# Ten output groups of the second layer turned back from channel rows instead of straight into token rows

## What is computed

```python
# first layer
xm = x * rsqrt(mean(x*x) + 1e-6) * rms_w * (1 + scale) + shift      # scale, shift = cond @ w_cond
q, k, v = split(xm @ w_qkv);  q, k = rope(q), rope(k)
x = softmax(q k^T / 4) v @ w_out + x
# second layer
xn = layer_norm(x) * norm_w + norm_b
q, k, v = xn @ q_w + q_b, xn @ k_w + k_b, (xn @ v_w + v_b) * mask
y = softmax(q k^T + (mask - 1) * 1e6) v
e = silu(cond) @ emb_w + emb_b
h = layer_norm(y) * sb_w + sb_b, times (1 + scale), plus shift
x = x + silu(h) @ out_w + out_b
```

## Time and profile before

| what | value |
|---|---|
| median of 3 runs | 493.06 us (492.68 to 494.52) |
| profiled execution, its own time | 493.28 us |
| its span in the trace | 491.5 us |
| PE, DVE, ACT, POOL busy | 479.5, 386.1, 342.7, 314.2 us |
| granted clock of PE | full speed in all 40 slices |

### The profile page before, as it was taken

One profiled execution on the slowest core, in us unless ns is written; L12 is line 12 of the kernel. 1 busy time (PEld: TensorE's weight loads), 2 busy tenths in 40 slices (PEclk: granted clock), 3 DMA queues, 4 the chain that ended last, 5 costly groups with the idle time before them and its releaser, 6 DMA issues.

```text
span 491.5 us, 9721 instructions
## 1 busy us (share of the span) xinstructions
PE 479.5 (98%) x3205; PEld 178.4 (36%) x3205; DVE 386.1 (79%) x990; ACT 342.7 (70%) x676; POOL 314.2 (64%) x447
## 2 busy tenths in 40 slices
PE   7999899999999999999999999999999999999996
PEld 3563322323333334333343234333333323333234
DVE  3767896998886688856887688967899999999224
ACT  1662467898767786867767776776787778777853
POOL 6569976888798898699737692739991055005501
PEclk9999999999999999999999999999999999999999
DMA  7775157444423365225412361104411121111011
GB/s 244 197 206 194 45 135 264 112 115 149 112 66 115 111 183 149 68 68 140 123 54 67 107 187 44 46 24 126 114 45 44 45 88 45 44 45 45 2 43 43
DMA packets 41577, 49.79 MB, mean 101 GB/s; under 512 B 12388, under 2 KB 34036, under 8 KB 41272
## 3 DMA queue, kind: packets, MB, share of 16 engines
q1 hardware_dynamic: 33336, 31.84, 22.6%
q0 software_dynamic: 7904, 16.03, 10.9%
q10 hardware_dynamic: 288, 1.31, 0.8%
HBM read 27.62 MB, written 19.01 MB: 95 GB/s over the span
## 4 chain that ended last, share of the span: by engine, by line
PE 79%; DVE 14%; issue 3%; POOL 2%; ACT 1%; DVEq 0%; POOLq 0%; ACTq 0%
PE bank L602 20%; PE bank L648 12%; PE bank L576 11%; PE bank L585 11%; PE bank L564 9%; DVE masked L958 8%; PE bank L659 6%; PE bank L676 5%; DVE row_max L961 2%; PE bank L633 2%; ACT probs L787 1%; PE bank L617 1%; PE bank L610 1%; PE bank L734 1%; POOL shift L1335 1%
## 5 line engine op out<-in xcount | busy, mean ns | idle before, releaser
L787 ACT ACTIVATE probs<-bank 128x512 f32<-128x512 f32 x512 | 270.2, 599 | 71.3 <-PE bank L576 70.6
L961 DVE TENSOR_REDUCE row_max<-bank 128x1 f32<-128x512 f32 x256 | 159.9, 681 | 38.1 <-PE bank L585 37.9
L585 PE MATMUL bank<-k_s,q_s 64*128 64x512 f16 x512 | 179.9, 382 | 2.1 <-DVE row_max L961 1.2
L958 DVE CUSTOM_DVE_ANT_0 masked<-bank,mask_bias 128x512 bf16<-128x512 f32 x256 | 162.1, 687 | 20.3 <-PE bank L585 19.6
L564 PE MATMUL bank<-q_s,k_s 64*128 64x512 f16 x512 | 151.3, 380 | 0.3
L576 PE MATMUL bank<-shift,kx 64*128 64x512 f16 x512 | 148.7, 376 | 0.0
L602 PE MATMUL bank<-probs,v_aug 128*17 128x512 f32 x1024 | 135.4, 598 | 0.7 <-ACT probs L787 0.7
L585 PEld LDWEIGHTS bank<-k_s,q_s 64*128 64x128 f16 x512 | 46.2, 93 | 154.6 <-DVE row_max L961 67.4
L1238 POOL TENSOR_SCALAR scaled<-row_max 128x16 f32<-128x16 f32 x30 | 7.7, 256 | 86.3 <-DVE row_max L958 49.0
L648 PE MATMUL bank<-xT,wqkv 128*128 128x512 f32 x128 | 59.6, 605 | 1.0 <-DVE xT L1095 0.6
L576 PEld LDWEIGHTS bank<-shift,kx 64*128 64x128 f16 x512 | 46.9, 95 | 33.4
(11 more groups left out here) (122 smaller groups left out, 480.6 us busy)
## 6 DMA issues: line engine op xcount, KB each, us to landing
q_s<-q_parts SPq DMA_DIRECT2D x32, 256.0 KB, 3.3
k_s<-k_parts SPq DMA_DIRECT2D x32, 256.0 KB, 4.4
k_parts<-parts POOLq DMA_DIRECT2D x62, 128.0 KB, 3.2
q_parts<-parts POOLq DMA_DIRECT2D x60, 128.0 KB, 3.0
X<-in_x SPq DMA_DIRECT2D x4, 512.0 KB, 7.1
O<-oT SPq DMA_DIRECT2D x64, 32.0 KB, 2.0
...
```

The lines of the kernel that those rows point to most:

```text
L585: nc.tensor.matmul(bank, m.q_s[slot][rows, i, queries], m.k_s[slot][rows, i, :], start=True, stop=True).then_inc(q.d_made, 1)
L787: act.activation(m.probs[k][:, h, :], bank, ACT.Exp, scale=1.0 if s >= B * NG else float(DH) ** -0.5)\
L958: dve.tensor_tensor_reduce(m.masked[D["max", n, k, h] % ND][:, :], bank, m.mask_bias[:, b, :], 1.0, LOWEST, ALU.add, ALU.max, to)\
L961: dve.tensor_reduce(to, bank, AX.X, ALU.max).then_inc(q.d_done, 1)
```

## The change

Groups 16 to 25 (`SENT` = 26) now take the first layer's path. Their `turn_output` and `write_output` go away. SP sends sums, raw output and inverses for them too; the reciprocal of groups 16 to 25 is taken by POOL, as a power of -1 of 128x16 numbers (`invert`), and POOL divides each finished chunk in place. Then PE turns the chunk into token rows (`turn_back`, four transposes, a piece `("back", b, c)`), and ACT empties the bank into `m.tokens`, which takes the place of `m.O` and lies in the room of the loaded condition weights. Five chunks are turned back: (0,0), (0,1), (1,0), (1,1), (2,0). The `f1` turns and the `y` pieces of batches 0 and 1 move one step later. POOL's list in the second layer is written anew.

Smaller edits: the second product with `chosen` becomes four transposes, and DVE adds the four partial columns in a reduction (`by_chunk`); POOL finishes `e`. ACT normalises the fourth of the first token tiles. POOL's first fill of `kx` waits for the modulation. In the first layer POOL rotates batch 3's first part between the two divisions of batch 0, and sends the second part before it normalises.

```diff
+SENT = LAYER + NG * (B - 2) + NG // 2
...
-PIECES[20] = ((), qk(1, LAST, 2, 3), (), v(1, LAST)[:1])
-PIECES[21] = (v(1, LAST)[1:], (), (), ())
-PIECES[22] = (*one(turn("f1", 0)), (), ())
-PIECES[23] = ((), (), y(1, 0)[:1], ())
-PIECES[24] = ((), (), (), y(1, 0)[1:])
-PIECES[26] = (*one(turn("f1", 1)), (), ())
-PIECES[27] = ((), (), y(1, 1)[:1], ())
-PIECES[28] = ((), (), (), y(1, 1)[1:])
+
+PIECES[20] = ((), qk(1, LAST, 2, 3) + (("back", 0, 0),), (), v(1, LAST)[:1])
+PIECES[21] = (v(1, LAST)[1:], (), (("back", 0, 1),), ())
+PIECES[23] = (*one(turn("f1", 0)), (), (("back", 1, 0),))
+PIECES[24] = ((), (), y(1, 0)[:1], ())
+PIECES[25] = ((), (), (("back", 1, 1),), y(1, 0)[1:])
+PIECES[27] = (*one(turn("f1", 1)), (), (("back", 2, 0),))
+PIECES[28] = ((), (), y(1, 1)[:1], ())
+PIECES[29] = ((), (), (), y(1, 1)[1:])
...
-for _b in range(B - 1):
-    STATISTICS[20 + NG * _b, 3] = ("f1", _b, None)
+for _b, _s in enumerate((21, 25, 28)):
+    STATISTICS[_s, 3] = ("f1", _b, None)
...
-        if op == "output" and k == 2 and s > LAYER:
+        if op == "output" and k == 2 and s > SENT:
             yield op, s - 1
-        if op == "output" and k == 3 and 0 < s <= LAYER:
+        if op == "output" and k == 3 and 0 < s <= SENT:
             yield "sums", s - 1
...
+        m.tokens = [m.wc[:, 2 * i:2 * i + 2, :].rearrange("p k n -> p (k n)").rearrange("p (t c) -> p t c", c=C)
+                    for i in range(2)]
...
+    def turn_back(piece):
+        _, b, c = piece
+        bank = a_free(A[piece])
+        pe.wait_ge(q.divided, normalised(B + b, c))
+        for t in range(TPB):
+            last = nc.tensor.transpose(bank[:, t * P:(t + 1) * P], m.raw[b % 2][:, c, t * P:(t + 1) * P], m.ident[:, :])
+        last.then_inc(q.a_made, 1)
...
-            pe.wait_ge(q.chosen_step, B)
+            pe.wait_ge(q.ident_made, 4)
             pe.wait_ge(q.a_done, A[kind, 0] + 1)
             for c in range(KC):
-                last = nc.tensor.matmul(bank[:, c * B:(c + 1) * B], m.conditions[:, c * P:(c + 1) * P], m.chosen[:, :],
-                                        start=True, stop=True)
+                last = nc.tensor.transpose(bank[:, c * P:(c + 1) * P], m.conditions[:, c * P:(c + 1) * P], m.ident[:, :])
...
-        if s > LAYER:
+        if s > SENT:
             act.wait_ge(q.d_made, D["output", s - 1] + 1)
...
+    def back(piece):
+        _, b, c = piece
+        bank = made(A[piece])
+        if b >= 2:
+            act.wait_ge(q.xn_made, TPB * NORMAL.index(("f1", b - 2)))
+        act.activation(m.tokens[b % 2][:, :, c * P:(c + 1) * P], bank.rearrange("p (t n) -> p t n", n=P), ACT.Copy)\
+            .then_inc(q.a_done, 1)
...
+            if piece == ("modulate", 0):
+                act.wait_ge(q.rstd0_made, 1)
+                act.activation(m.XN[0][:, TPB - 1, :], m.X[:, TPB - 1, :], ACT.Copy,
+                               scale=m.rstd["p0"][:, TPB - 1:TPB]).then_inc(q.xn0_made, 1)
...
-            dve.wait_ge(q.d_done, D["output", NG * (B + b) + NG - 1] + 1)
-            statistics(kind, b, lambda t: m.O[b % 2][:, t, :], 0, TPB)
+            dve.wait_ge(q.a_done, max(A[piece] for piece in A if piece[:2] == ("back", b)) + 1)
+            if NG * (B + b) + NG > SENT:
+                dve.wait_ge(q.d_done, D["output", NG * (B + b) + NG - 1] + 1)
+            statistics(kind, b, lambda t: m.tokens[b % 2][:, t, :], 0, TPB)
...
-        for t in range(TPB):
+
+        for t in range(TPB - 1):
             normal_tile(dve, m, "p0", m.X[:, 0:TPB, :], m.XN[0], t, t).then_inc(q.xn0_made, 1)
...
+    def by_chunk(bank):
+
+        return bank.rearrange("p (c k w) -> p c w k", k=KC, w=W32)[:, :, 0:B, :]
...
+        dve.tensor_reduce(m.mod0[:, :, :], by_chunk(made(D["modulate", 1])), AX.X, ALU.add).then_inc(q.mod_made, 1)
...
+        dve.tensor_reduce(m.e[:, :, :], by_chunk(made(D["embed", 1])), AX.X, ALU.add).then_inc(q.d_done, 1)
...
-        if op == "sums":
+        if op == "sums" and at[0] < LAYER:
             invert(*at)
...
+    def divide(pu, c):
+
+        layer, b = divmod(pu, B)
+        pool.wait_ge(q.output_out, group_out(NG * pu + 2 * c + 1))
+        pool.wait_ge(q.inv_in[c], 32 * (pu + 1))
+        to = raw = m.raw[b % 2][:, c, :]
+        if layer == 0:
+            use = USES.index(("f0", b))
+            await_read(pool, q, use - 2)
+            to = m.xT[use % 2][:, c, :]
+        pool.tensor_tensor(to, raw, m.inverse[c][:, :], ALU.mult).then_inc(q.divided, 1)
+
+    def invert(s):
+
+        pool.wait_ge(q.sums_in, 16 * (s + 1))
+        pool.wait_ge(q.inv_out, 16 * s)
+        pool.tensor_tensor(m.inv_sum[:, :, :, :].rearrange("p t h w -> p (t h w)"), m.sums[:, :], m.minus_one[:, :],
+                           ALU.pow).then_inc(q.inv_made, 1)
...
     divide(0, 0)
+    rotate(3, 0)
     divide(0, 1)
-    rope(3, 0, 7)
-    rope(3, 1, send=False)
+    rotated_parts(3, 0, 7)
+    rope(3, 1)
...
-    send_parts(3, 1)
...
+        if b == 2:
+            pool.wait_ge(q.one_made, 1)
+            invert(LAYER)
         add_bias(b, 0)
         divide(b + 1, 1)
         negate(NG * b + 11)
         if b == 1:
             modulation()
+    invert(LAYER + 1)
     normalise(LAST)
+    divide(B, 0)
     add_output_bias(LAST)
     add_bias(LAST - 1, 1)
+    invert(LAYER + 2)
     negate(NG * LAST + 9)
-    for i in range(4):
+    for i in range(2):
         split(B + LAST, i)
-
-    for b in range(LAST):
-        negate(NG * (B + b) + 6)
-        rstd("f1", b)
-        normal("f1", b)
-        if b == 0:
-            add_bias(LAST, 0)
-        negate(NG * (B + b) + 7)
-        if b == 0:
-            add_bias(LAST, 1)
+    invert(LAYER + 3)
+    for i in range(2, 4):
+        split(B + LAST, i)
+
+    def silu(b):
         for h in range(CT):
             i, h = silu_ready(pool, q, ("turn", "f1", b, h))
             pool.tensor_scalar(m.tanh[h], m.tanh[h], 1.0, None, ALU.add).then_inc(q.tanh_step, 1)
             pool.wait_ge(q.tanh_step, CT * b + h + 1)
             pool.tensor_tensor(m.xT[i][:, h, :], m.tanh[h], m.halved[h], ALU.mult).then_inc(q.silu_made, 1)
-        for n in (NG * (B + b) + 8, NG * (B + b) + 9):
-            if n in POOL_SHIFTS:
-                negate(n)
+
+
+    for b in range(2):
+        n = NG * (B + b)
+        negate(n + 6)
+        divide(B + b, 1)
+        invert(n + 4)
+        if b == 0:
+            add_bias(LAST, 0)
+        negate(n + 7)
+        rstd("f1", b)
+        normal("f1", b)
+        invert(n + 5)
+        if b == 0:
+            add_bias(LAST, 1)
+        negate(n + 8)
+        divide(B + b + 1, 0)
+        silu(b)
+        if b == 0:
+            invert(n + 6)
+        negate(n + 9)
+        if b == 0:
+            invert(n + 7)
+    negate(GROUPS - 2)
+    rstd("f1", 2)
+    normal("f1", 2)
+    negate(GROUPS - 1)
+    silu(2)
...
-        if b >= 2:
+        if b >= B + 2:
+            sp.wait_ge(q.a_made, A["back", b - 2 - B, g // 2] + 1)
+        elif b >= 2:
             sp.wait_ge(q.divided, normalised(b - 2, g // 2))
...
-        if 0 < s <= LAYER:
+        if 0 < s <= SENT:
             sums(s - 1)
```

More of the change, by code:

```diff
@@ L283, in chunk_rows, with normalised @@
     return slice(G * DH * (g % 2), G * DH * (g % 2 + 1))
-def normalised(b, c):
-    return CT * b + c + 1
+def normalised(pu, c):
+    return CT * pu + c + 1
 def await_shift(engine, q, n):
@@ L759, in tensor @@
                 turn_tokens(piece)
+            if piece[0] == "back":
+                turn_back(piece)
             if piece[0] == "qk":
@@ L823, in tokens @@
             act.wait_ge(q.mod_made, CT)
-            act.activation(to, bank, ACT.Identity, bias=m.mod0_shift[:, h, b:b + 1], scale=m.mod0_scale[:, h, b:b + 1])\
+            act.activation(to, bank, ACT.Identity, bias=m.mod0[:, CT + h, b:b + 1], scale=m.mod0_scale[:, h, b:b + 1])\
                 .then_inc(q.a_done, 1)
@@ L916, in scalar @@
                 tokens(piece)
+            if piece[0] == "back":
+                back(piece)
             if piece[0] == "qk":
@@ L982, in write_output @@
         bank = made(D["output", s]).rearrange("p (t h w) -> p t h w", t=KT, h=G)
-        if s == LAYER:
-            dve.wait_ge(q.inv_out, 16 * LAYER)
-        if g == 0 and pu < B + 2:
-            dve.wait_ge(q.divided, normalised(pu - 2, CT - 1))
-        if g == 0 and pu >= B + 2:
+        if s == SENT:
+            dve.wait_ge(q.inv_out, 16 * SENT)
+        if s == SENT or g == 0:
             dve.wait_ge(q.xn_made, TPB * NORMAL.index(("f1", pu - 2 - B)))
-        if s > LAYER:
+        if s > SENT:
             dve.wait_ge(q.d_done, D["output", s - 1] + 1)
@@ L1213, in normal @@
             await_turned(pool, q, NORMAL[n - 2])
-        src = m.O[b % 2] if kind == "f1" else m.X[:, TPB * b:TPB * b + TPB, :]
+        src = m.tokens[b % 2] if kind == "f1" else m.X[:, TPB * b:TPB * b + TPB, :]
         for t in range(TPB):
@@ L1262, in split, with rotate @@
         send_parts(pu, i)
-    def rope(b, i, *shifts, send=True):
+    def rotate(b, i):
```

(12 more changed lines are left out.)

54 lines of the change are left out of this document (27 added, 27 removed).

## The result

| | before | after |
|---|---|---|
| median | 492.87 us (492.66 to 494.52, 4 runs) | 506.82 us (506.58 to 509.75, 4 runs) |
| ratio, 95% interval | | 1.0292 (1.0254 to 1.0330) |
| span of the profiled execution | 491.5 us | 505.1 us |

The change makes the kernel 13.95 us slower. The prediction was 495.0 us with a range of 487.9 to 498.5; the time lies above the range.

A forecast was written before the change was run, and what follows sets the result against it. PE's own list was taken to bound the kernel; the profiled 493.28 us less 5.1 of gains plus 7.0 of waits gave 495.2, set to 495.0 us because that execution lay 0.2 above the median. Range 487.9 to 498.5.

The forecast's parts named there:

- DVE-limited tiles fall to their price: Steps 22 to 28: without ten write-outs on DVE, four tiles about 0.3 us too long fall to plain price, −1.2 us.
- length of the power: POOL's 128x16 power takes 3.0 us, carried on from the 4-column and 2-column rows; lower bound 1.04.
- step 18: At `y` of batch 3, PE waits 2.4 us for POOL's division, with group 16's inverse ahead; lower bound 0.4.
- shift 22: In step 21, another inverse of 3.0 us between POOL's splits makes PE wait 1.0 us; lower bound none.
- shift 24: In step 23, POOL's list takes 22.3 us against PE's 21.8, so PE waits 0.5 us; lower bound none.
- shift 25: In step 24, POOL needs 12.7 us and PE 10.6, so PE waits 2.1 us; lower bound none.
- chunk (1,1): In step 25, the division ends 15.2 us after shift 25, PE comes after 14.2: wait 1.0 us, lower bound none.
- Rival 1: POOL's 16-column power stays near 1.04 us, leaving only 0.4 us of waits: 488.4 us, chance 0.33.
- SP's small transfer takes about 2.0 us: In step 18, group 16's sums go from `oT` ready at 290.53 to 292.5, when its inverse can start.
- The way through memory of (1,0): Step 24: the inverse's write to read 1.4 us, to the division 4.6, some 0.4 before: 6.4 in all.
- rival 2: In steps 20 to 25, the inverses' write and read each lose about 1.2 us: +3.5, 498.5 us, chance 0.21.
- the likeliest case: Whole kernel: 5.1 us of gains, 7.0 us of PE's waits for POOL, 495.0 us, own range 493 to 497, chance 0.46.

The follow-up runs named there:

- run with 0.21 us: The changed kernel with POOL's power of -1 replaced by a multiplication of the same shape, leaving out the reciprocal of groups 16 to 25; 493.91 us.
- filler run: The changed kernel with twenty idle products on PE directly before its wait for the division of batch 3 in step 18; 503.73 us.
- sums-first run: The changed kernel with SP sending the sums of the last group before the operands of group s+3 in every step; 502.34 us.

## Why the prediction was wrong

| step of the prediction | predicted us | measured us |
|---|---|---|
| PE's turns and chunks | −2.9 | −2.9 (taken from the records' prices) |
| opening, step 3, step 7 | −1.04 | −1.35 (tile of step 7 at 148.06, before 149.41) |
| DVE-limited tiles fall to their price | −1.2 | −1.2, but two plain tiles at +1.67 and two others at +0.3 |
| length of the power | 3.0 | 2.93 |
| step 18 | +2.4 | +7.26 |
| shift 22 | +1.0 | +1.06 |
| shift 24 | +0.5 | +0.72 |
| shift 25 | +2.1 | +3.36, and +1.60 in the tile behind |
| chunk (1,1) | +1.0 | +1.12 |

The measured column sums to −5.45 + 3.9 + 15.1 = +13.6 us, the difference of the spans.

The mechanism was right: POOL with ten powers of 3 us becomes late, in these places. Three of the five waits were right to 0.3 us. For shifts 22 and 24 that was no luck, their tiles hardly change between the kernels with powers whose PE order is the same there (3.53 to 3.57 and 3.79 to 3.90 us). For chunk (1,1) it was in part, as that tile varies by 0.8. Rival 1 (the width hardly matters) is refuted by the 2.93 us row. A power costs POOL about 0.16 us a column, (2929 − 1039)/12 ns. The rate in the Trainium skill, GPSIMD Engine Reference, section 3.1, is given for an addition. Carried to a power it led to 1.07 us, and the trace has 1.86 us more. Where the rival would have ended at best can be read from the run with 0.21 us: 493.9, not 488.4.

These steps failed; with 2.8, 3.7, 3.9 and 1.3 us they make 11.7 of the 11.8 us between 495.0 and 506.8:

- *"SP's small transfer takes about 2.0 us"* in step 18. It took the duration of the undisturbed 32 KB row for a transfer issued in the same 3 us as two operand loads and four of POOL's transfers. It was 4.80 to the inverse's start. The row was there: POOL's `k_parts` at 289.88 stands in the earlier trace rows beside ACT's copy at 289.93.
- *A wait costs its own length.* The prediction had no term for PE's clock. The step-18 wait left it at 1.2 GHz for +2.06 us, and the shift-25 wait for most of the 1.60 in the tile behind. The first is shown by the filler run. For the second, the `y` tile takes 4.41 in the sums-first run and 4.44 without powers, where the clock stayed up, and 5.9 to 6.0 in all six kernels where it fell.
- *"DVE ... the four tiles of 0.3 us should fall to their plain price: −1.2."* It weighed the ten write-outs taken away, had no term for the statistics that move by one step, and called the `y` pieces' move by one a mere change of place. Two statistics thereby left a tile with a piece of PE for a plain one, at 1.67 us each. The prices were in the profile: DVE's four maxima fill 2.45 of a plain tile's 2.48.
- *The way through memory of (1,0), "6.4 in all"*: 7.5 from the end of the inverse (375.96) to the division, and shift 25 comes 1.3 later than predicted. That looks like rival 2's mechanism at work beside the likeliest case, not in its place, but chunk (0,1), which rival 2 had late, took its plain 3.07. And in four other kernels with powers the same tile was 2.0 to 2.5 us too long, as predicted: this step failed in the profiled execution, and why it varies stays open. Treated as exclusive cases, none of the three reached 506.

Of step 18's 4.86 us too much, 2.06 is the clock and 2.8 the sums; the earlier copy of `oT` and the earlier arrival of PE, both 1.2 to 1.3 us, cancel. Two sums of the prediction are slightly off without changing anything here: POOL's list before shift 24 adds up to 22.2 us, not 22.3, and rival 2's three delays to 3.7, not 3.5.
